# An order table of rounds for TensorE and VectorE in a fused attention and expert kernel

## The chip, the cores and the metric

The kernel runs on one core of one Trainium2 chip. The metric is the device time of one launch in microseconds, median of several runs. A profiled execution of the same program, in which the trace is recorded, stands beside it.

## What is computed

A batch of eight sequences of 1024 rows by 256 columns goes through a layer norm without weights, then through attention (16 heads of 16, rotary position) and through a layer of 8 experts in which each expert picks its own rows.

```python
def reference(x, ...):
    xn = _layernorm(x)
    return x + attention(xn, ...) + experts(xn, ...)

def attention(x, ...):
    z = layernorm(x) * ln_w + ln_b
    q, k, v = z @ Wq.T + bq, z @ Wk.T + bk, z @ Wv.T + bv      # heads of 16
    q, k = rope(q), rope(k)
    attn = softmax(q @ k.T / sqrt(16))
    return x + (attn @ v) @ Wo.T + bo

def experts(x, ...):
    affinity = softmax(x @ gate_w)                # 8 experts
    gating, index = top_k(affinity.T, 256)        # per sequence and expert
    h = silu(x[index] @ Wg) * (x[index] @ Wu)
    return zeros.at[index].add((h @ Wd) * gating)
```

## The kernel before

The program is written engine by engine, without a scheduler: each engine has its own list, and semaphores hold them together. A prologue prepares batch 0 (q, k, v and the routing for sequence 0). Then `attend` runs once for each of the eight sequences (batches here), and the experts follow in 32 units of 512 rows.

Within batch b, attention is 64 **steps** of two **pairs**. Step s has head group s // 16 (four heads), query half (s // 8) % 2 and key tile s % 8. A score pair is two matmuls, for two heads in two row lanes of the array (L985); it fills one of three `score` banks (RING), so pair p may be written only when the exponential of pair p - 3 is done. ScalarE takes one exponential per pair (L777, 1024 in all). The value product of a step (`weigh`, L999) multiplies all four heads' exponentials by the values and a column of ones; it is four matmuls, eight records in the trace. Eight steps accumulate in the only `o_ps` bank. After the eighth, VectorE copies it to `o_sb` (`copy_o`, L1475), and step 8k waits for that copy.

The order is counted in **cycles** of two steps. Cycle c issues scores of step 2c, product 2c - 2, scores of step 2c + 1, product 2c - 1; with a long job (q/k, v, output projection) in the cycle the two products go together between the scores. The products run two steps behind, so the last two of a batch are issued in cycle 0 of the next.

Between them TensorE prepares the next batch and finishes the previous one through **jobs**, each into the one `side` bank, from which VectorE takes it before the next job may start (`pe.wait_ge(side_free, jobs.before(job))`):

- ("z", half, c): four transposes of the normed rows (L852), ready when VectorE's norm3 is;
- ("logits", half) the router's logits (L859); ("square", half) head norms (L890) of squares that GpSimd makes (L667); ("peak",) a turn of the peaks (L899);
- ("qk", half, k) q and k projections (L868, six matmuls); ("v", pair) (L878); ("wo", quarter) the output projection of the previous batch (L909).

`NEXT_JOBS` and `PREV_JOBS` are dictionaries from a cycle to its job, 25 jobs a batch; batch 0 has no "wo" jobs, and `LAST_JOBS` has few, since no batch follows.

VectorE walks the same cycles (L1531). For the next batch it does, for each half, norm1 (first statistics, L1128, L1132), norm2 (`xn`, L1157 to L1137), stats2, norm3 (moments and `z`, L1173 to L1137); between them GpSimd raises the variance to the power -1/2 (L645). Later it does rotary products (L1261), rotary (L1277), split (high and low part of q and k, L1323, L1325). For the previous batch it does invert and the quarter splits (L1352 to L1495). All of it stands in one list with `copy_o` and the drains of the jobs. In the last batch VectorE runs 96 operations of top-k instead (`take_top`), four or five a cycle.

If a sequence's scores could overflow, a branch (`wide`) computes maxima first. It is not taken in this run.

Of the kernel before, what the change touches and what calls it, by code (L numbers as in the profile page):

```python
# [15 lines left out]
P = 128  # L16
# [100 lines left out]
def program(nc, ctx, g):  # L117
# [118 lines left out]
    def rows_ps(t):  # L236
# [65 lines left out]
    NEXT_JOBS = {4: ("z", 0, 0), 5: ("z", 0, 1), 6: ("logits", 0),  # L302
# [3 lines left out]
    SECOND_JOBS = {c + (c < 9): job for c, job in NEXT_JOBS.items()}  # L306
    PREV_JOBS = {9: ("wo", 0), 15: ("wo", 1), 23: ("wo", 2), 30: ("wo", 3)}
    LAST_JOBS = {0: ("top",), 9: ("wo", 0), 15: ("wo", 1), 23: ("wo", 2), 28: ("lists",), 30: ("wo", 3)}
    LONG_JOBS = ("qk", "v", "wo")
    END_JOBS = (("wo", 0), ("wo", 1), ("wo", 2), ("wo", 3))  # L310
    NFIRST, NNEXT = len(FIRST_JOBS), len(NEXT_JOBS) + len(PREV_JOBS)


    class Jobs:


        def __init__(self, base, by_cycle, order=None):
            self.base, self.by_cycle = base, by_cycle
            order = order or [by_cycle[c] for c in sorted(by_cycle)]
            self.offset = {job: i for i, job in enumerate(order)}  # L320
# [10 lines left out]
    def jobs_of(b):  # L331
# [3 lines left out]
        base = b * NNEXT + (NFIRST + len(NEXT_JOBS) - NNEXT)  # L335
        if isinstance(b, int) and b == NB - 1:
            return Jobs(base, LAST_JOBS)
        return Jobs(base, {**NEXT_JOBS, **PREV_JOBS})
# [12 lines left out]
    first_jobs = FirstJobs(0, None, FIRST_JOBS)  # L351
    NACT = sum(by_act(job) for job in FIRST_JOBS)
    last_jobs = jobs_of(NB - 1)
    end_jobs = Jobs(last_jobs.base + len(LAST_JOBS), None, END_JOBS)
# [490 lines left out]
    def _(pe):  # L845
# [48 lines left out]
        def turn_peaks(bank, n):  # L894
            pe.wait_ge(v_peaked, n + 1)
# [77 lines left out]
        def scores(b, s):  # L973
            hg, qh, kt = s // (2 * KT), (s // KT) % 2, s % KT
            par = hg % 2
            if b == 0 and s == KT // 2:
                pe.wait_ge(late_in[1], STACK_DMA // 2)
            elif b == 0 and s == KT:
                pe.wait_ge(late_in[0], STACK_DMA // 2)
            for i in range(NPAIR):  # L980
                p = NPAIR * s + i
                need(pe, exp_done, b * PAIRS + (p - RING + 1))
                for w in range(LANES):
                    rows = slice(w * LANE, w * LANE + FULL)
# [730 lines left out]
```

## Time and profile before

| | us |
|---|---|
| median of 3 runs | 1713.04 |
| lowest, highest | 1712.26, 1714.15 |
| span of the profiled execution | 1713.7 |
| busy in it: TensorE | 1667.3 (97%) |
| ScalarE | 1190.4 (69%) |
| VectorE | 1075.3 (63%) |
| GpSimd | 508.9 (30%) |
| first to last attention exponential | 59.5 to 1130.0 |

The profiled execution is 0.7 us above the median. Busy time of TensorE counts overlapping records, so that a share of 97% does not mean that it works at its peak; the chain of waits says what it waits for. In rows of the timeline and of groups, "x8" is the number of instructions, the figure before it the time that they cover.

### The profile page before, as it was taken

What the parts mean: (1) busy time and instruction counts of PE and PEld (TensorE: products, weight loads), DVE (VectorE), ACT (ScalarE), POOL (GpSimd) and SP (SyncE); (2) the same over time, 40 slices, a digit from 0 to 9 for tenths busy, and PEclk for the clock granted to TensorE, in tenths of its full rate; (3) what the DMA queues carried; (4) which work ended last, traced back from release to release, by engine and by line L of the source; (5) the groups of instructions that cost most, each with busy time, mean ns of one, the idle gap of its engine ahead of it and who ended that gap; (6) DMA issues with size and microseconds to landing.
All of it is one profiled execution on the core that took longest, in us unless ns stands there. A gap on an engine that the chain in (4) does not pass through costs nothing.

```text
span 1713.7 us, 29029 instructions
## 1 busy us (share of the span) xinstructions
PE 1667.3 (97%) x11128; PEld 947.8 (55%) x11128; DVE 1075.3 (63%) x2351; ACT 1190.4 (69%) x1416; POOL 508.9 (30%) x479
## 2 busy tenths in 40 slices
PE   5799999999999999999999999999999999999997
PEld 4234334333434433434434433368888888888886
DVE  7875487577477567558558658866555555454543
ACT  4698998998899899899898899953333333343322
POOL 3112101201111111112112100036566565656553
PEclk9799999999999999999999999999999999999999
DMA  5634754674574475465474566345444443534332
GB/s 168 173 60 122 162 116 106 174 145 106 134 169 122 115 156 143 116 142 138 118 161 104 118 134 140 59 152 117 86 93 66 92 92 66 99 62 96 65 56 31
DMA packets 113987, 196.08 MB, mean 114 GB/s; under 512 B 20896, under 2 KB 59680, under 8 KB 113696
## 3 DMA queue, kind: packets, MB, share of 16 engines
q1 hardware_dynamic: 83696, 143.01, 36.5%
q0 software_dynamic: 29040, 49.83, 15.0%
q8 instruction: 105, 1.72, 0.4%
q10 hardware_dynamic: 1088, 1.05, 0.2%
q14 instruction: 58, 0.48, 0.1%
HBM read 117.27 MB, written 76.55 MB: 113 GB/s over the span
## 4 chain that ended last, share of the span: by engine, by line
PE 93%; DVE 4%; DMA 1%; POOL 1%; issue 1%; ACT 0%; POOLq 0%; ACTq 0%; DVEq 0%
PE o_ps L999 28%; PE score L1079 20%; PE score L985 20%; PE side L868 5%; PE score L1091 5%; PE o_ps L1091 3%; PE side L878 3%; PE side L909 3%; PE side L1091 2%; PE score L1066 2%; PE side L852 1%; DMA probs<-in_wo_t 1%; PE side L859 0%; PE side L890 0%; POOL out L689 0%
## 5 line engine op out<-in xcount | busy, mean ns | idle before, releaser
L777 ACT ACTIVATE probs<-score 128x1024 f32<-128x1024 f32 x1024 | 967.8, 1063 | 105.5 <-PE score L985 103.3
L999 PE MATMUL o_ps<-probs,v_ones 128*32 128x512 f32 x4096 | 524.9, 605 | 1.8 <-DVE o_sb L1475 1.5
L985 PE MATMUL score<-q_stack,k_stack 50*128 50x512 f32 x2048 | 395.8, 458 | 4.0 <-issue 3.4
L985 PEld LDWEIGHTS score<-q_stack,k_stack 50*128 50x128 f32 x2048 | 164.0, 185 | 352.2 <-ACT probs L777 310.7
L761 ACT ACTIVATE probs<-score 128x512 f32<-128x512 f32 x128 | 76.6, 598 | 328.9 <-PE score L1079 328.9
L689 POOL DMA_INDIRECT out<-probs,rot x128 | 203.4, 1589 | 207.6 <-DVE probs L1440 178.3
L1425 DVE TENSOR_TENSOR probs<-score,probs 128x512 f32<-128x512 f32 x128 | 88.5, 691 | 205.3 <-PE score L1079 179.3
L999 PEld LDWEIGHTS o_ps<-probs,v_ones 128*32 128x32 f32 x4096 | 92.3, 108 | 201.1 <-issue 140.1
L667 POOL TENSOR_TENSOR square<-qk 128x512 bf16<-128x512 f32 x56 | 77.3, 1409 | 387.5 <-DVE qk L1278 387.5
L1079 PE MATMUL score<-k_stack,q_stack 128*128 128x512 f32 x640 | 158.6, 390 | 0.0
L678 POOL DMA_INDIRECT qk<-xn_rows,rot x128 | 132.0, 1031 | 38.3 <-issue 29.3
L1079 PE MATMUL score<-k_stack,zn_hi 128*128 128x512 f32 x512 | 139.9, 390 | 0.0
L1079 PEld LDWEIGHTS score<-k_stack,q_stack 128*128 128x128 f32 x640 | 119.1, 188 | 24.1
L1475 DVE COPY o_sb<-o_ps 128x512 f32<-128x512 f32 x64 | 44.3, 692 | 125.3 <-PE o_ps L999 125.3
L643 POOL TENSOR_SCALAR ve<-mv 128x4 f32<-128x4 f32 x32 | 8.3, 261 | 352.6 <-DVE mv L1132 352.6
L1079 PEld LDWEIGHTS score<-k_stack,zn_hi 128*128 128x128 f32 x512 | 95.0, 188 | 19.8 <-issue 0.8
L755 ACT CAST parts<-probs 128x512 fp32r<-128x512 f32 x128 | 78.6, 614 | 33.3 <-DVE probs L1425 33.3
L659 POOL COPY v_ones<-v_sb 128x512 f32<-128x512 f32 x32 | 19.7, 616 | 162.9 <-DVE v_sb L1347 85.9
L1417 DVE TENSOR_TENSOR w_hi<-probs,parts 128x512 fp32r<-128x512 f32 x96 | 65.4, 681 | 0.0
L1347 DVE TENSOR_TENSOR v_sb<-side,bv_sb 128x256 f32<-128x256 f32 x56 | 21.0, 416 | 68.9 <-PE side L878 68.9
L1440 DVE TENSOR_SCALAR probs<-score,rot 128x256 f32<-128x256 f32 x64 | 30.7, 483 | 52.1 <-PE score L1091 52.1
L1179 DVE COPY moments_of<-stats 32x2 f32<-32x2 f32 x224 | 46.2, 206 | 3.4
(282 smaller groups left out, 2546.9 us busy)
## 6 DMA issues: line engine op xcount, KB each, us to landing
q_parts<-parts SPq DMA_DIRECT2D x16, 1024.0 KB, 4.3
k_parts<-parts SPq DMA_DIRECT2D x16, 1024.0 KB, 7.4
q_stack<-q_parts SPq DMA_DIRECT2D x62, 256.0 KB, 7.2
k_stack<-k_parts SPq DMA_DIRECT2D x62, 256.0 KB, 8.7
q_stack<-q_parts SPq DMA_DIRECT2D x66, 128.0 KB, 7.6
k_stack<-k_parts SPq DMA_DIRECT2D x66, 128.0 KB, 8.3
o_sums<-o_sb SPq DMA_DIRECT2D x256, 32.0 KB
num<-o_sums SPq DMA_DIRECT2D x32, 256.0 KB
```

Source lines behind the costliest of these rows:

```text
L667: last = pool.tensor_tensor(square[i][:, :], qk[:, i, :], qk[:, i, :], ALU.mult)
L678: pool.indirect_dma_start(xs[par][:, t, :], None, xn_dram[:, :], bass.IndirectOffsetOnAxis(ap=rows_now[bp][:, t:t + 1], axis=0))\
L689: pool.indirect_dma_start(out[:, :], bass.IndirectOffsetOnAxis(ap=rows_now[bp][:, t:t + 1], axis=0), y[par][t], None, compute_op=ALU.add)\
L755: act.copy(h_hi[:, f, :], h[f % 2]).then_inc(h_high, 1)
L761: act.activation(silu[f % 2], g_ps[f % 2], ACT.Silu).then_inc(silu_done, 1)
L777: act.activation(probs[probs_of(b, s)][:, 2 * i:2 * i + 2, :], score[ring_of(b, p)][:, :, :], ACT.Exp, scale=SCALE).then_inc(exp_done, 1)
L868: last = pe.matmul(bank[:, :], wt[:, c, a * P:(a + 1) * P], zt[:, c, th * HALF:(th + 1) * HALF], start=i == 0 and c == 0, stop=i == 2 and ...
L985: last = pe.matmul(score[ring_of(b, p)][:, w, :], k_stack[par][rows, i, kt * P:(kt + 1) * P], q_stack[par][rows, i, qh * HALF:(qh + 1) * H ...
L999: last = pe.matmul(o_ps[j * KEYS_W:(j + 1) * KEYS_W, :], v_ones[par][:, kt, j, :], probs[probs_of(b, s)][:, j, :], start=kt == 0, stop=kt ...
L1079: last = pe.matmul(bank[f % 2], wt[k][w][:, c, f * P:(f + 1) * P], xt[:, c, :], start=i == 0 and c == 0, stop=i == 2 and c == DC - 1)
L1091: last = pe.matmul(rows_ps(t), ht, wt[k][DOWN][:, f, :], start=i == 0 and f == 0, stop=i == 2 and f == FC - 1)
L1425: dve.tensor_tensor(h[f % 2], u_ps[f % 2], silu[f % 2], ALU.mult).then_inc(h_done, 1)
```

## The change

One table replaces the cycles on both engines. An entry is a **round**: so many score pairs, so many products, and at most one job, issued in this order. Products still run two steps behind at a batch's start (LAG = 2), and 54 rounds make a batch.

```diff
-    NEXT_JOBS = {4: ("z", 0, 0), 5: ("z", 0, 1), 6: ("logits", 0),
-                 7: ("qk", 0, 0), 8: ("qk", 0, 1), 10: ("qk", 0, 2), 12: ("qk", 0, 3), 14: ("z", 1, 0), 16: ("z", 1, 1), 17: ("logits", 1), 18: ("square", 0),
...
+    NEXT_ROUNDS = ((3, 2), (2, 1), (3, 1), (1, 1), (3, 2), (3, 1, ("z", 0, 0)), (2, 1), (2, 1, ("z", 0, 1)), (3, 2),
+                   (2, 0, ("logits", 0)), (2, 2), (3, 0, ("qk", 0, 0)), (2, 2), (3, 2), (2, 0, ("qk", 0, 1)),
+                   (3, 2, ("wo", 0)), (3, 2), (3, 0, ("qk", 0, 2)), (2, 2), (3, 0, ("qk", 0, 3)), (0, 1), (3, 2),
...
+    FIRST_LATER = {("z", 0, 0): 7, ("z", 0, 1): 9, ("logits", 0): 10}
...
+            LAST_ROUNDS.append((NPAIR, 1, *{1: (("top",),), 57: (("lists",),)}.get(s, ())))
...
-    LOW_CYCLE = (28, 29, 30)
+    LOW_CYCLE = (29, 30, 31)
...
-    ROUTER_CYCLE = (9, 19)
+    ROUTER_CYCLE = (9, 20)
```

The rest of the table goes on in the same way: rounds of two or three pairs with two products, and rounds of two or three pairs with a job and no product. In all there are 38 groups of products (14 of one, 22 of two, 2 of three) where there were 48, and 51 groups of pairs (29 of three, 19 of two, 3 of one). Batch 0 takes the table without "wo" and with its first three jobs later; the last batch has rounds of two pairs and one product. TensorE:

```diff
-                scores(b, 2 * c)
-                grouped = c in jobs.by_cycle and jobs.by_cycle[c][0] in LONG_JOBS
-                weigh_past(b, 2 * c - 2, prev)
...
+            p, s = 0, -LAG
+            for entry in rounds_of(b):
+                for p in range(p, p + entry[0]):
+                    if p % GROUP_PAIRS == 0:
+                        open_group(b, p // GROUP_PAIRS, wide)
+                    score_pair(b, p)
+                p += entry[0] > 0
+                for s in range(s, s + entry[1]):
+                    weigh_past(b, s, prev)
+                s += entry[1] > 0
+                job = job_in(entry)
+                if job is not None:
                     pe.wait_ge(side_free, jobs.before(job))
                     run_job(jobs, job, nxt, prev, side[:, :])
```

VectorE walks the same rounds: in each, the copies of the output halves that end in it, then what belongs to the cycles whose first pair is in it, then the job's drain. Its work for the second half moves a cycle later (products 21 to 22, rotary 22 to 23, split 22 and 24 to 23 and 25), the peak of the values is taken in two halves, one scaling replaces two in `limits`, and the copy of the previous batch's last output half goes ahead of norm1.

```diff
+                for done in steps:
+                    if done >= 0 and done % KT == KT - 1:
+                        copy_o(b, done // KT)
+                    elif done == -1 and prev is not None:
                         copy_o(prev, 2 * NG - 1)
-                    stats2(nxt, 0)
...
+                for c in (at // (2 * NPAIR) for at in pairs if at % (2 * NPAIR) == 0):
+                    if nxt is None:
+                        alongside_last(b, prev, c)
+                    else:
+                        alongside(b, nxt, prev, jobs, c)
```

**VectorE at the start of a middle batch.** `xin` to `z` is the norm chain of the next batch, `o_sb<-o_ps` the copy of an output half. Before:

```order
L1128 BN_STATS stats<-xin 128x6 x4
L1132 BN_AGGR mv<-stats 128x2 x4
L1157 TENSOR_SCALAR grown<-rstd 128x4
L1158 SCALAR_TENSOR_TENSOR offset<-mv,rstd 128x4
L1137 TENSOR_SCALAR xn<-xin,mv,rstd 128x256 x4
L1475 COPY o_sb<-o_ps 128x512
L1128 BN_STATS stats<-xn 128x6 x4
```

Now:

```order
L1517 COPY o_sb<-o_ps 128x512
L1170 BN_STATS stats<-xin 128x6 x4
L1174 BN_AGGR mv<-stats 128x2 x4
L1199 TENSOR_SCALAR grown<-rstd 128x4
L1200 SCALAR_TENSOR_TENSOR offset<-mv,rstd 128x4
L1179 TENSOR_SCALAR xn<-xin,mv,rstd 128x256 x4
L1170 BN_STATS stats<-xn 128x6 x4
```

The copy has moved from behind norm2 to the head of the list.

**TensorE where step 47 ends an output half and step 48 begins the next,** in a middle batch, with buffer numbers (v_ones0 serves steps 32 to 47, v_ones1 steps 48 to 63). Before:

```order
L999 MATMUL o_ps<-probs1,v_ones0 32x512 x4
L999 MATMUL o_ps<-probs2,v_ones0 32x512 x4
L985 MATMUL score0<-q_stack1,k_stack1 128x512 x2
L985 MATMUL score1<-q_stack1,k_stack1 128x512 x2
L878 MATMUL side<-w_hi2,zn_hi 128x256 x2
L878 MATMUL side<-w_lo2,zn_hi 128x256 x2
L878 MATMUL side<-w_hi2,zn_lo 128x256 x2
```

Now:

```order
L1026 MATMUL score0<-q_stack1,k_stack1 128x512 x2
L1026 MATMUL score1<-q_stack1,k_stack1 128x512 x2
L1040 MATMUL o_ps<-probs2,v_ones0 32x512 x4
L1040 MATMUL o_ps<-probs0,v_ones1 32x512 x4
L1026 MATMUL score2<-q_stack1,k_stack1 128x512 x2
```

The two products on either side of the border, which had scores and a v job between them, now follow each other. The same holds for steps 23 and 24 and for 39 and 40.

**VectorE around the job ("z", 1, 1)** of a middle batch. Before:

```order
L1475 COPY o_sb<-o_ps 128x512
L1200 COPY xnT<-side 128x512
L1201 TENSOR_SCALAR znT<-side,lnw_sb,lnb_sb 128x512
L1207 CAST zn_hi<-znT 128x2x512
L1213 TENSOR_TENSOR zn_lo<-znT,zn_hi 128x2x512
```

Now:

```order
L1242 COPY xnT<-side 128x512
L1243 TENSOR_SCALAR znT<-side,lnw_sb,lnb_sb 128x512
L1249 CAST zn_hi<-znT 128x2x512
L1255 TENSOR_TENSOR zn_lo<-znT,zn_hi 128x2x512
L1517 COPY o_sb<-o_ps 128x512
```

The copy after step 31 has moved from ahead of the drain of the z job, with its two casts, to behind it.

## Rows read from the trace of the kernel before

**Rows 1.** Busy time by stretch: batch 0, a middle batch (3), the last; columns in the first line

```profile
core 0: us, PE busy (x) PEld busy (x) DVE busy (x) ACT busy (x) POOL busy (x), PEclk, DMA share, GB/s
59.48:194.86 135.38, 133.31 (x914) 49.64 (x915) 86.81 (x210) 121.03 (x130) 22.70 (x26) 0.96 0.52 119
466.39:602.17 135.78, 135.78 (x976) 55.17 (x972) 89.77 (x219) 121.68 (x132) 22.34 (x25) 1.00 0.57 134
1009.46:1129.96 120.50, 119.22 (x820) 39.19 (x812) 99.40 (x219) 118.37 (x129) 10.00 (x11) 1.00 0.48 103
```

**Rows 2.** The chain of waits, cycles 4 to 9 of batch 3: start us, length us, what

```profile
487.57 0.59 PE side L852 x4
...
490.48 1.00 PE o_ps L999 x8
...
491.91 0.66 PE score L985 x4
492.57 1.85 PE o_ps L999 x16
...
495.09 1.59 PE side L868 x6
...
504.63 1.57 PE side L909 x12
```

**Rows 3.** The chain of waits, cycle 2 of batch 3

```profile
476.33 0.84 PE score L985 x4
```

**Rows 4.** VectorE's timeline, start of batch 3: start, length, work, [idle before <-releaser]

```profile
464.18 1.41 DVE L1128 BATCH_NORM_STATS2 stats<-xin 128x6 f32<-128x256 f32 x4 [0.29 <-issue]
...
467.49 0.17 DVE L1157 TENSOR_SCALAR grown<-rstd 128x4 f32<-128x4 f32 x1 [1.49 <-POOL rstd L645]
...
476.89 1.38 DVE L1137 TENSOR_SCALAR z<-xn,mv,rstd 128x256 f32<-128x256 f32 x4
```

**Rows 5.** Timelines of TensorE and VectorE where batch 5's first output half is copied

```profile
739.47 1.06 PE L999 MATMUL o_ps<-probs,v_ones 128*32 128x512 f32 x8
...
741.34 1.06 PE L999 MATMUL o_ps<-probs,v_ones 128*32 128x512 f32 x8
...
740.60 0.69 DVE L1475 COPY o_sb<-o_ps 128x512 f32<-128x512 f32 x1 [0.70 <-PE o_ps L999]
```

**Rows 6.** VectorE's timeline, the drain of a second z job

```profile
488.19 0.69 DVE L1200 COPY xnT<-side 128x512 f32<-128x512 f32 x1 [2.46 <-PE side L852]
...
490.36 1.23 DVE L1213 TENSOR_TENSOR zn_lo<-znT,zn_hi 128x1024 fp32r<-128x1024 f32 x1
```

**Rows 7.** VectorE's timeline from a quarter split to norm3 and the rotary products

```profile
499.87 0.88 DVE L1352 SCALAR_TENSOR_TENSOR base<-base,grown,bo_sb 128x256 f32<-128x256 f32 x2
...
502.45 0.74 DVE L1252 TENSOR_SCALAR qk<-side,bq_sb 128x512 f32<-128x512 f32 x1
...
515.42 0.68 DVE L1261 TENSOR_TENSOR rot<-qk,cos_sb 128x512 f32<-128x512 f32 x1
```

**Rows 8.** Start of batch 0: TensorE and VectorE timelines, and busy time with PEclk

```profile
80.80 1.28 PE L999 MATMUL o_ps<-probs,v_ones 128*32 128x512 f32 x8 [1.49 <-DVE o_sb L1475]
...
78.77 1.38 DVE L1137 TENSOR_SCALAR z<-xn,mv,rstd 128x256 f32<-128x256 f32 x4
...
80.66 3.90 DVE L1194 TENSOR_REDUCE gate_sum<-base 128x8 f32<-128x2048 f32 x1
...
81.00:85.00 4.00, 4.00 (x20) 0.70 (x12) 3.56 (x1) 2.44 (x3) 0.00 (x0) 0.57 1.00 242
```

**Rows 9.** SyncE's timeline (last load of batch 4's first stack), and the page's DMA issues

```profile
585.51 0.42 SPq L461 DMA_DIRECT2D k_stack<-k_parts  x1
...
k_stack<-k_parts SPq DMA_DIRECT2D x62, 256.0 KB, 8.7
```

**Rows 10.** VectorE's timeline, the last batch: two top-k steps of eight

```profile
1013.45 0.69 DVE L1525 MAX8 top_gate<-znT 128x8 f32<-128x512 f32 x1
...
1015.77 0.69 DVE L1525 MAX8 top_gate<-znT 128x8 f32<-128x512 f32 x1
```

More of the change, by code:

```diff
@@ new lines, in first_rounds @@
+    def first_rounds():
+        moved = []
+        for r, entry in enumerate(NEXT_ROUNDS):
+            job = job_in(entry)
+            later = [j for j, at in FIRST_LATER.items() if at == r]
+            job = later[0] if later else None if job in FIRST_LATER or job is not None and job[0] == "wo" else job
+            moved.append(entry[:2] if job is None else (*entry[:2], job))
+        return moved
+    FIRST_ROUNDS = first_rounds()
+    NEXT_JOBS, SECOND_JOBS, LAST_JOBS = ([job_in(entry) for entry in rounds if len(entry) == 3]
+                                         for rounds in (NEXT_ROUNDS, FIRST_ROUNDS, LAST_ROUNDS))
@@ L1529, in take_top, with alongside, alongside_last @@
                 dve_t.mark(dve.match_replace(top_scores, top_gate[:, eight], top_scores, -1.0))
+        def alongside(b, nxt, prev, jobs, c):
+            if prev is not None:
+                splits = LAST_SPLIT_CYCLE if nxt is None else SPLIT_CYCLE
+                if c == 7:
+                    invert(prev, 1)
+                if c in splits:
+                    quarter_split(prev, splits.index(c))
+            elif c == 4:
+                sum_gate()
+            if c == 0:
+                norm1(nxt, 0)
+                norm2(nxt, 0)
+                stats2(nxt, 0)
+            elif c in (1, 10):
+                norm3(nxt, c // 10)
+            elif c == 6:
+                norm1(nxt, 1)
+            elif c == 9:
+                norm2(nxt, 1)
+                stats2(nxt, 1)
+            elif c in (11, 22):
+                products(jobs, c // 22, 0)
+            elif c in (12, 23):
+                rotary(0)
+            elif c in (14, 24):
+                products(jobs, c // 24, 1)
+            elif c in (15, 25):
+                rotary(1)
+            elif c in (28, 30):
+                value_peak(jobs, c // 30)
+            elif c == 31:
+                invert(b, 0)
+            if c in (13, 22):
+                affinities(nxt, c // 22)
+            if c in (13, 23):
+                split(nxt, c // 23, 0)
+            elif c in (15, 25):
+                split(nxt, c // 25, 1)
+        def alongside_last(b, prev, c):
+            if c == 7:
+                invert(prev, 1)
+            if c in LAST_SPLIT_CYCLE:
+                quarter_split(prev, LAST_SPLIT_CYCLE.index(c))
+            for op in range(TOPS_DONE[c], TOPS_DONE[c + 1]):
+                take_top(op)
+            if c == LISTS_CYCLE:
+                order_lists()
+            if c == 30:
+                invert(b, 0)
+            if c in LOW_CYCLE:
+                if c == LOW_CYCLE[0]:
+                    dve.wait_ge(parts_out, NB * 2 * PARTS_DMA)
+                first_cast(LOW_CYCLE.index(c))
+                low_weights(0, LOW_CYCLE.index(c))
         def attend(b, nxt, prev):
@@ L1597, in _ @@
+                job = job_in(entry)
+                if job is not None:
+                    take(jobs, job, nxt, prev, side[:, :])
         dve.memset(peaks[:, :], 0.0).then_inc(zeros_set, 1)
@@ L1649, in _ @@
         first("v", 3)
-        value_peak(first_jobs)
+        value_peak(first_jobs, 0)
+        value_peak(first_jobs, 1)
         first_low(1, 1)
```

177 lines of the change are left out of this document (69 added, 108 removed), and 3 rows, old and new, of tables (NEXT_JOBS, NEXT_ROUNDS).

## The prediction

> **What bounds the kernel now.** I read the stretches of the batches first. A middle batch takes 135.8 us, the first 135.4, the last 120.5 [rows 1]. In a middle batch TensorE is marked busy all the time, ScalarE for 121.7 us. Matmul records overlap, so that mark proves nothing by itself; the chain of waits does. In cycles 4 to 9 of batch 3 it runs through TensorE alone: two score pairs 0.66 us, one value product 1.00, two in one go 1.85, a projection job 1.59, and no exponential between them [rows 2]. TensorE's own order is the bound there. In the first cycles of a batch, which have no job, two pairs hold the chain for 0.84 us instead of 0.66 [rows 3]: ScalarE sets the pace there. That happens in eight or nine half cycles, 1.6 us a batch.
>
> Check by addition for a middle batch: 128 pairs by 0.33, 42.4; 32 single products by 1.00 and 16 double ones by 1.85, 61.6; eight q/k jobs by 1.59, four output jobs by 1.57, four v jobs of as many matmuls of the same size, and nine short jobs of at most 0.59, about 30; waits 1.6. Together 135.6, measured 135.8. So there is little to win: all that TensorE loses to others today is 1.6 us.
>
> **The parts, for a middle batch (1 to 6).**
>
> Fewer groups of products. A product that follows another costs 1.85 - 1.00 = 0.85 us instead of 1.00 [rows 2]. 48 groups become 38: 10 x 0.14 = **-1.4 us**. Score pairs cost 0.33 each in a group of two, and no row shows a third; bounds 0.33 (the pairs before it) and 0.13 (half the 0.26 us a matmul of the q/k job, since the two lanes run side by side). I take 0.33, the same operation, so groups of three give nothing. The Trainium skill (TensorE: Matmul & The Clock Gate, section Back-to-back issue gap) puts the gap of matmuls in a stream at N/2.4 + 2.5 ns, 216 ns for 512 columns; by it the third pair would save 0.12 us, 29 times, and the sum would be 3.4 us a batch lower. No pair in the trace is that cheap.
>
> The first z job. The copy of the last output half (step -1) now stands ahead of norm1 in VectorE's list. Today norm1 starts at 464.18, 2.2 us before the batch's first exponential [rows 1, 4], and z is done at 476.89 + 1.38 = 478.27: 14.1 us, of which 0.6 are the copy in between; one of two waits for GpSimd's powers is the 1.49. After the change the copy waits for step -1: three pairs (1.0), a first product (0.86), the second's 1.06 to its end, a semaphore (0.07), the copy (0.6). So norm1 starts 3.6 us after the batch's first score and z is ready at 3.6 + 13.5 = 17.1. TensorE comes to ("z", 0, 0) after 15 pairs (5.0), eight products in six groups (two of 1.85, four of 1.00: 7.7) and about 0.6 of exponential waits, at 13.3. Wait **+3.8** (3 to 4.3). Today the job stands in cycle 4, behind 20 pairs, and z is ready before it. Behind the waiting job stand only scores, so ScalarE runs dry too, but it has 14 us a batch to spare.
>
> Output halves that end inside a group. There is one o_ps, so step 8k starts only when VectorE has copied it after step 8k - 1. Today at least two pairs lie between. Where just these do, the rows show the shortest way: product at 739.47, copy 740.60 to 741.29, next product 741.34, 1.87 us from start to start [rows 5]. In the new order steps 23 and 24, 39 and 40, 47 and 48 stand in one group, where the second would start after 0.86. 1.87 - 0.86 = 1.0, three times: **+3.0**, and more where VectorE is busy at that moment. This is the surest term.
>
> Step 32. From the start of job ("z", 1, 1) TensorE has that job 0.59, a pair 0.33, steps 30 and 31 1.85, three pairs 1.0: 3.8 us to step 32. VectorE drains the job from 0.7 on, with both casts 3.4 [rows 6], and only then copies: 0.7 + 3.4 + 0.7 = 4.8. **+1.0** (0 to 1.2).
>
> ("qk", 0, 3) waits for the drain of ("qk", 0, 2). From the start of ("qk", 0, 1), TensorE needs 15.0 us to come to it: two q/k jobs (3.2), one output job (1.6), 14 pairs (4.6) and three double products (5.6). VectorE has just begun a quarter split then (499.87 to 502.45, 2.6), followed by a drain, norm2, stats2, wo's sum, norm3, another drain and the four rotary products (502.45 to 516.10, 13.6) [rows 7]; in the new order the products stand ahead of the second drain, so that this one ends last: 16.3. **+1.3** (0 to 2).
>
> The clock. In batch 0 TensorE stood idle for 1.49 us until 80.80, and over the next four microseconds (81 to 85) the granted clock was 0.57, most of it at 1.2 GHz instead of 2.4: 4 x 0.43 = 1.7 us lost [rows 8]. In a middle batch it is 1.00 throughout [rows 1]. The wait for z leaves TensorE idle for 3.5 us; I take the same drop behind it, **+1.7** (0 to 3.4).
>
> At nothing: the second half's products, rotary and split move one VectorE cycle later, so q and k of the next batch go out through SP's queue up to 4 us later. The last load of the next first stack is issued at 585.51 and takes 8.7 us [rows 9], the batch's first exponential is at 602.17: 8 us of cover. If it were gone the batch would start late. GpSimd's squares come later by as much, and so does their job. The peak of the values in halves, and one scaling instead of two, lie on an idle VectorE.
>
> Sum: -1.4 + 3.8 + 3.0 + 1.0 + 1.3 + 1.7 = **+9.4** a batch, +56 in six.
>
> Batch 0: no previous copy, so z is done at 80.15 as now. gate_sum (cycle 4, 3.90 us) now stands ahead of the copy after step 7, so that one ends at 84.7 and step 8 starts then instead of at 80.80 [rows 8], with one short job more behind it: +3.4. Then the borders 3.0, step 32 0.9, two drains 3, exponentials where no output job fills the time 2, groups -1.4: **+11**.
>
> Last batch: VectorE's copies now follow cycle 4k's five top-k operations, 2.32 us for three [rows 10], 3.9 us a cycle against 3.7 of TensorE's pace. Waits of 1 to 2 us at steps 8, 24 and 40, partly caught up: **+3** (0 to 5). The experts stay.
>
> 56 + 11 + 3 = +70 on the profiled 1713.7; the median is 0.7 lower than that span, so **1783 us**.
>
> **Rivals.**
> 1. Faster: VectorE's copy and z are not what comes last. TensorE keeps the -1.4, and spread jobs win back the 1.6 of exponential waits: -3.0 x 6, 1695 us. It decides whether step 24 starts 0.86 us after step 23 and z comes before 13.3 us. For it: VectorE is busy only 90 us of 136. Against: the copy needs step 8k - 1, and no free VectorE makes the 1.87 shorter.
> 2. The same waits, but the clock stays: 7.7 x 6 + 14 = +60, 1773.
> 3. Only what the order itself forces: z 3.0, borders 3.0, groups -1.4, so 4.6 x 6 + 5 = +33, 1746. VectorE's lateness elsewhere would have to vanish.
> 4. A third pair is cheap: if the array runs on once a group streams, at 0.21 instead of 0.33, 3.4 us a batch come back, 24 in all: 1759. Against it every pair of the trace. It is also what the skill's figure above would give.
> 5. VectorE falls behind in earnest, borders cost 1.5 each and stacks land late: over 1802.
>
> **Numbers.** Forecast 0.50, rival 2 0.22, rival 3 0.08, rival 4 0.04, rival 5 0.07, rival 1 0.06, and 0.03 that gains and waits cancel within 0.2%, about what a measurement can tell from no change. The range 1745 to 1802 holds the forecast, 2, 3, 4 and the bounds. Faster 0.06, same 0.03, slower 0.91.
>
> **What would show it.** A middle batch of 143 to 146 us, the surplus in four places: TensorE idle some 3.5 us about 13 us into each batch, ended by VectorE's z; three times 1.0 us of o_ps waiting for the copy; a clock under 1.0 just after the z wait; the q/k drain at about 52 us. The last batch 121 to 125. The prediction is wrong if z is ready at 13 us, if the copies end before TensorE asks, or if three pairs take under 0.9 us.

## The result

| | us | against the kernel before |
|---|---|---|
| before, median of 4 runs | 1713.51 (1712.26 to 1714.15) | |
| changed, median of 4 runs | 1781.43 (1776.49 to 1784.46) | ratio 1.0388, 95% interval 1.0375 to 1.0400 |
| changed, profiled execution | 1782.51, span 1780.4 | |

The change makes the kernel 68 us slower. Busy time by stretch of the changed kernel, cut where each batch issues its first exponential, as in [rows 1]: batch 0, batch 3, the last batch, the experts behind it.

```profile
core 0: us, PE busy (x) PEld busy (x) DVE busy (x) ACT busy (x) POOL busy (x), PEclk, DMA share, GB/s
56.67:206.85 150.18, 134.73 (x910) 53.30 (x907) 85.32 (x202) 121.26 (x130) 22.49 (x24) 0.92 0.47 107
495.71:638.95 143.24, 134.21 (x976) 56.35 (x972) 90.55 (x220) 121.38 (x131) 22.62 (x24) 0.99 0.56 127
1068.94:1194.08 125.14, 121.31 (x822) 39.53 (x820) 98.57 (x219) 119.07 (x128) 9.56 (x11) 0.97 0.46 99
1194.08:1780.36 586.28, 570.88 (x3392) 504.19 (x3392) 303.74 (x501) 198.15 (x342) 334.08 (x281) 0.99 0.43 84
```

Batch 0 is 14.8 us longer, batch 3 7.5, the last 4.6. Batches 1 to 6 together are 47.5 us longer (8.9, 8.4, then 7.5 to 7.6 four times). ScalarE has the same work, 121.4 us in batch 3; TensorE has the same instructions, but its busy time fell from all of the batch to 134.2 of 143.2. For the rest it now stands still. The page of the profile says for whom: the lines of its costliest groups over the whole run, with the idle time before them at the end of a line.

```profile
L819 ACT ACTIVATE probs<-score 128x1024 f32<-128x1024 f32 x1024 | 968.5, 1040 | 173.2 <-PE score L1026 169.0
L1040 PE MATMUL o_ps<-probs,v_ones 128*32 128x512 f32 x4096 | 521.6, 611 | 28.7 <-DVE o_sb L1517 28.7
```

Before, ScalarE's exponentials stood idle for 105.5 us in all and the products for 1.8. TensorE in batch 3, by groups with idle time; then its timeline at the places of [rows 5] and of the sum:

```profile
L1040 PE MATMUL o_ps<-probs,v_ones 128*32 128x512 f32 x512 | 64.3, 607 | 3.4 <-DVE o_sb L1517 3.4
L1026 PE MATMUL score<-q_stack,k_stack 50*128 50x512 f32 x260 | 46.3, 444 | 0.4 <-ACT probs L819 0.2
L910 PE MATMUL side<-zn_hi,w_hi 128*128 128x512 f32 x16 | 5.8, 446 | 1.4 <-DVE qk L1294 1.4
```

```profile
495.11 0.97 PE L1026 MATMUL score<-q_stack,k_stack 50*128 50x512 f32 x6
...
507.30 1.07 PE L1040 MATMUL o_ps<-probs,v_ones 128*32 128x512 f32 x8
512.23 0.63 PE L894 MATMUL side<-ident_sb,z 128*128 128x128 f32 x4 [3.86 <-DVE z L1179]
...
549.73 0.73 PE L910 MATMUL side<-zn_hi,w_hi 128*128 128x512 f32 x2 [1.38 <-DVE qk L1294]
...
553.21 1.07 PE L1040 MATMUL o_ps<-probs,v_ones 128*32 128x512 f32 x8
555.09 1.07 PE L1040 MATMUL o_ps<-probs,v_ones 128*32 128x512 f32 x8 [0.81 <-DVE o_sb L1517]
```

The first z job waits 3.86 us for VectorE, from 13.3 to 17.1 us after the batch's first score at 495.11. ("qk", 0, 3) waits 1.38 for the drain of ("qk", 0, 2). Steps 23 and 24 start 1.88 us apart instead of 0.86, with the copy between them; steps 39/40 and 47/48 do the same, and step 32 comes 0.84 us late. VectorE at the start of the batch, which answers to [rows 4]:

```profile
498.00 0.69 DVE L1517 COPY o_sb<-o_ps 128x512 f32<-128x512 f32 x1 [1.91 <-PE o_ps L1040]
498.61 1.39 DVE L1170 BATCH_NORM_STATS2 stats<-xin 128x6 f32<-128x256 f32 x4
...
510.70 1.38 DVE L1179 TENSOR_SCALAR z<-xn,mv,rstd 128x256 f32<-128x256 f32 x4
```

Norm1 follows the copy, and z is done 13.5 us after norm1 began, as the prediction had it. The clock behind that wait, by stretch: in the 4 us of waiting TensorE was busy for 0.77 us at full clock, then it worked at half of it.

```profile
509.00:513.00 4.00, 0.77 (x6) 0.63 (x8) 3.03 (x15) 0.86 (x1) 0.00 (x0) 1.00 1.00 154
513.20:516.40 3.20, 3.20 (x16) 0.70 (x12) 1.10 (x2) 1.94 (x2) 0.00 (x0) 0.50 1.08 233
```

One thing in the chain of waits is cheaper than the prediction took it. Start, length, work, around 560 and 611 us:

```profile
558.40 0.90 PE score L1026 x6
...
563.90 0.66 PE score L1026 x4
...
611.80 2.71 PE o_ps L1040 x24
```

Three pairs hold TensorE for 0.90 us, two for 0.66: the third costs 0.24, not 0.33. Three products take 2.71, each further one 0.86.

### The profile page after: what moved, and what is told of

Same layout as the page of the kernel before. It is cut to its first block, busy times and chain, and to the rows that moved or that the text cites. A ratio compares the mean times of both kernels' runs of the same rounds, so it can differ in the third digit from the quotient of the medians.

```text
span 1780.4 us, 29029 instructions
## 1 busy us (share of the span) xinstructions
PE 1664.7 (94%) x11128; PEld 960.4 (54%) x11128; DVE 1079.8 (61%) x2351; ACT 1190.0 (67%) x1416; POOL 515.4 (29%) x479
## 4 chain that ended last, share of the span: by engine, by line
PE 74%; DVE 18%; ACT 3%; issue 2%; POOL 2%; DMA 1%; another core or an unknown queue 0%; ACTq 0%; POOLq 0%; DVEq 0%
PE o_ps L1040 20%; PE score L1121 19%; PE score L1026 13%; PE score L1133 5%; PE side L910 4%; PE o_ps L1133 3%; DVE moments_of L1221 3%; PE side L920 3%; PE side L1133 2%; ACT probs L819 2%; DVE o_sb L1517 2%; DVE stats L1170 2%; PE side L951 2%; PE score L1108 1%; POOL rstd L687 1%
## 5 line engine op out<-in xcount | busy, mean ns | idle before, releaser
L1026 PE MATMUL score<-q_stack,k_stack 50*128 50x512 f32 x2048 | 377.9, 453 | 9.8 <-ACT probs L819 4.2
L1026 PEld LDWEIGHTS score<-q_stack,k_stack 50*128 50x128 f32 x2048 | 170.5, 189 | 316.7 <-ACT probs L819 249.1
L1040 PEld LDWEIGHTS o_ps<-probs,v_ones 128*32 128x32 f32 x4096 | 97.9, 109 | 253.5 <-issue 140.3
L1121 PE MATMUL score<-k_stack,zn_hi 128*128 128x512 f32 x512 | 140.2, 390 | 1.2 <-DVE probs L1467 1.2
L1517 DVE COPY o_sb<-o_ps 128x512 f32<-128x512 f32 x64 | 44.2, 690 | 134.7 <-PE o_ps L1040 131.7
L701 POOL COPY v_ones<-v_sb 128x512 f32<-128x512 f32 x32 | 25.2, 787 | 194.9 <-DVE v_sb L1389 111.9
L1294 DVE TENSOR_SCALAR qk<-side,bq_sb 128x512 f32<-128x512 f32 x28 | 21.0, 748 | 61.8 <-PE side L910 61.8
```

The lines of the kernel that those rows point to most:

```text
L1026: last = pe.matmul(score[ring_of(b, p)][:, w, :], k_stack[par][rows, i, kt * P:(kt + 1) * P], q_stack[par][rows, i, qh * HALF:(qh + 1) * H ...
L1040: last = pe.matmul(o_ps[j * KEYS_W:(j + 1) * KEYS_W, :], v_ones[par][:, kt, j, :], probs[probs_of(b, s)][:, j, :], start=kt == 0, stop=kt ...
L1121: last = pe.matmul(bank[f % 2], wt[k][w][:, c, f * P:(f + 1) * P], xt[:, c, :], start=i == 0 and c == 0, stop=i == 2 and c == DC - 1)
L1517: dve.tensor_copy(o_sb[il % 2][:, :], o_ps[:, :]).then_inc(o_copied, 1)
```

## The experiments

The theory: four kinds of waits that the new order puts on TensorE, and the clock behind one of them, make the 68 us. Rivals: the walk of a table costs by itself; the waits are VectorE's lateness and would stand elsewhere; filled time comes back as waits for exponentials. Each kernel ran beside the kernel before on its chip (medians there 1712.7 to 1715.4); batch lengths come from its one profiled execution.

**e1, the old order in the new code.** The table of the middle batches spells out the old cycles, and a helper fills the tables of batch 0 and of the last batch in the same way. VectorE's work goes back to its old cycles too, but for a few operations: the copy ahead of norm1, the value peak in two halves and the one scaling stay as changed. The 11128 matmuls of TensorE come in the order of the kernel before.

```diff
+    def by_cycles(at):
+        rounds = []
+        for c in range(STEPS // 2):
+            job = at.get(c)
+            both = job is not None and job[0] in ("qk", "v", "wo")
+            rounds += [(2, 2 if both else 1), (2, 0 if both else 1) + (() if job is None else (job,))]
+        return rounds
```

> The changed kernel with its table filled so that TensorE issues exactly the order of the kernel before (every matmul in the same place); the walk through a table, the value peak in two halves and VectorE's copy of the last product group ahead of the norm stay as the change has them. Theory (the order of the rounds costs the 68 us): 1713 us within 4, middle batches at 135.7 us as before, against 143.3 with the new table; the copy ahead of norm1 may hold z back by about 1 us, but the z job stands behind cycle 4 there and has that time. Rival (the table's code, or VectorE's new order, costs by itself): 1745 us or more, middle batches at 140 or more.

Measured: 1717.69 us (10 runs), ratio 1.0015 (1.0006 to 1.0025). Busy time of batch 3:

```profile
464.28:600.04 135.76, 135.76 (x976) 55.20 (x972) 90.05 (x219) 121.67 (x132) 21.58 (x24) 1.00 0.59 134
```

Batches take 135.3, 135.8 six times and 120.5, the old lengths to 0.1 us, though VectorE's copy stands ahead of norm1 here too and norm1 starts at 467.56, 3.3 us into the batch:

```profile
467.56 1.39 DVE L1179 BATCH_NORM_STATS2 stats<-xin 128x6 f32<-128x256 f32 x4
```

The table, its code and the early copy cost the batches nothing: where the job stands in cycle 4, z has the time. The loss lies in the two orders that e1 puts back, that of the rounds and that of VectorE's other work along them. e1 does not tell these two apart; e4, and batch 0 of e7, do. The median is 2.5 us above the kernel beside it, clear of the noise. In the profile that time stands outside the batches, which together are 0.2 us shorter than before.

**e2, the z jobs later.** In rounds 7, 9 and 10 in place of 5, 7 and 9 (only the entries that change, out of their lines):

```diff
-                   (3, 1, ("z", 0, 0)), (2, 1), (2, 1, ("z", 0, 1)), (3, 2), (2, 0, ("logits", 0)), (2, 2),
+                   (3, 1), (2, 1), (2, 1, ("z", 0, 0)), (3, 2), (2, 0, ("z", 0, 1)), (2, 2, ("logits", 0)),
```

> In the table of the middle batches the jobs z(0,0), z(0,1) and the first logits move from rounds 5, 7 and 9 to rounds 7, 9 and 10, where batch 0 has them already; all else stays. Theory (TensorE comes to z 3.9 us too early, 12.2 us into a batch where z is there at 17.1, and its clock then falls to 0.5 for 3.4 us, worth 1.6 us): the wait of 4.9 us falls to 1.6 or less, the stretch at clock 0.5 goes, and a drain wait of up to 1.5 us in front of qk(0,0) may come: 2.5 to 5.5 us less for each of the six middle batches, 15 to 33 in all, 1757 us (1748 to 1766). Rival (the time before z is filled with work that is missing later, so exponentials or the copy end the next wait): the same 1781 within 4. Rival (the clock falls without the wait as well): z's part alone, 10 to 15 us, 1769.

Measured: 1758.46 us, 1.0250 (1.0233 to 1.0267). TensorE's groups in batch 3 that wait for VectorE, then the z jobs:

```profile
L910 PE MATMUL side<-zn_hi,w_hi 128*128 128x512 f32 x16 | 5.8, 446 | 2.7 <-DVE znT L1262 1.4 <-DVE qk L1294 1.4
L894 PE MATMUL side<-ident_sb,z 128*128 128x128 f32 x16 | 2.6, 287 | 0.0
```

The wait for z is gone, the clock stays at 1.00, and 1.4 us came back in front of ("qk", 0, 0), which now stands right behind the logits: middle batches 140.1, 3.2 less (3.9 and 1.5 come back and 1.4 goes; of the 0.8 left the trace marks 0.2 as a wait for an exponential, the rest is open). Batch 0 and the last batch have the same instructions as in the changed kernel and took 151.0 and 122.7 us against 150.2 and 125.1; so the lengths of those two differ by 1 to 2 us from one execution to the next.

**e3, the borders.** At steps 23/24, 39/40 and 47/48 the last product of an output half and the first of the next go to different rounds, in batch 0 too (only the entries that change):

```diff
-(0, 1), (3, 2)
+(0, 2), (3, 1)
-(3, 3), (3, 0, ("qk", 1, 1)), (2, 2)
+(3, 2), (3, 0, ("qk", 1, 1)), (2, 3)
-(2, 2), (2, 0, ("v", 0))
+(2, 1), (2, 0, ("v", 0)), (0, 1)
```

> Three entries of the table are cut so that no two products of one round lie on both sides of a product group's end (steps 23 and 24, 39 and 40, 47 and 48): the first product of the new group goes to the next round, with a round of score pairs between. Theory (TensorE waits 1.0 us at each of the three for VectorE's copy of the finished group): three waits of 1.0 us go in each of the seven batches with this table, less up to 1 us of waits for exponentials that come in their place: 2 to 3 us per batch, 14 to 21 in all, 1765 us (1760 to 1769). Rival (the copy is late because VectorE is busy, wherever the product stands): no more than 5 us, 1776 to 1781.

Measured: 1768.87 us, 1.0307 (1.0289 to 1.0324), 12.6 less than the changed kernel. Batches 3 and 4 and the waits of batch 4:

```profile
487.49:630.14 142.65, 135.85 (x976) 57.22 (x972) 90.63 (x220) 120.86 (x131) 22.60 (x24) 0.98 0.57 129
630.14:771.24 141.10, 134.30 (x976) 56.73 (x972) 90.51 (x220) 120.87 (x131) 22.59 (x24) 0.99 0.55 127
```

```profile
L1040 PE MATMUL o_ps<-probs,v_ones 128*32 128x512 f32 x512 | 64.0, 608 | 0.9 <-DVE o_sb L1517 0.9
```

The wait for the copy falls from 3.4 to 0.9 us (step 32's is left), 2.2 us a batch where the clock was low for 3.4 us as before. In four of the six the low stretch behind z lasted 6.8 us and took 1.5 of it back. The time is in the expected range, the gain of 12.6 us just under its 14 to 21, the mechanism the expected one.

**e4, VectorE's order alone.**

```diff
+                late = NPAIR if nxt is None else 0
-                for c in (at // (2 * NPAIR) for at in pairs if at % (2 * NPAIR) == 0):
+                for c in (at // (2 * NPAIR) for at in pairs if at % (2 * NPAIR) == late):
...
-            elif c == 4:
+            elif c == 5:
                 sum_gate()
```

> Two orders on VectorE alone, TensorE's table untouched: in the last batch the top-k, the splits and the low weights of a cycle come one round later, so behind the copy of a product group that ends there and not ahead of it; in batch 0 the sum of the gate (3.9 us) moves from cycle 4 to cycle 5, behind the first copy. Theory (the walk of the table puts these ahead of the copies: waits of 1.3, 1.6 and 1.2 us before steps 8, 24 and 40 of the last batch, 1.9 us before step 8 of batch 0): the last batch falls from 125.1 to 121.5, batch 0 from 150.2 to 148.3, total 1776 us. Rival (the last batch is longer since its wo jobs come one cycle later): last batch stays at 125, total 1779 to 1781.

Measured: 1776.18 us, 1.0353 (1.0335 to 1.0370). Batch 0 and the last batch:

```profile
56.42:204.55 148.13, 135.50 (x910) 53.32 (x907) 85.52 (x202) 121.33 (x130) 22.47 (x24) 0.93 0.48 109
1065.12:1185.33 120.21, 119.97 (x822) 39.44 (x820) 98.79 (x219) 118.42 (x128) 9.54 (x11) 1.00 0.48 103
```

2.1 and 4.9 us less: the last batch is back at its old length, with its output jobs where the change put them. Its loss was the top-k ahead of the copies. The products of the last batch, in the changed kernel and in e4, and the clock behind the second of its three waits (1.09, 1.46 and 1.07 us):

```profile
L1040 PE MATMUL o_ps<-probs,v_ones 128*32 128x512 f32 x512 | 69.1, 618 | 3.6 <-DVE o_sb L1517 3.6
L1040 PE MATMUL o_ps<-probs,v_ones 128*32 128x512 f32 x512 | 67.4, 604 | 0.0
```

```profile
1120.50:1127.40 6.90, 6.90 (x32) 1.90 (x28) 6.66 (x16) 3.88 (x4) 0.00 (x0) 0.51 0.68 218
```

The same last batch, with the same three waits, took 122.7 us in e2, where the clock stayed, and 123.8 in e5, where it was low for 3.4 us; so by these some 2.5 us of the 4.9 are the waits and the rest is the clock. Of batch 0, the trace of e4 shows that the wait before step 8 is gone (1.6 us in the changed kernel, 2.1 in e2, 2.8 in e5). The 2.1 us of its length prove less, since e5, which leaves batch 0 alone, has 148.4 us too.

**e5, z one round later.** ("z", 0, 0) in round 6, nothing else.

> Only the job z(0,0) of the middle batches moves, by one round (5 to 6); z(0,1) and the logits stay in rounds 7 and 9. TensorE should come to it 1.7 us later than in the changed kernel (a single product and two pairs), about 14 us into the batch, so that a wait of 1.6 to 3.2 us stays before z, and qk(0,0) keeps its place behind the logits. Theory (a wait of 4.9 us on z takes the clock to 0.5; waits of about 1.8 us, as those before qk in the last study's runs, don't): the wait is 1.6 to 3.2 us, the clock stays at 1.0, the middle batches take 139.5 to 141 us and the whole about 1760 us (1755 to 1767). Rival (any wait on z takes the clock down): batches of 141.5 to 143, 1768 to 1778 us.

Measured: 1766.09 us, 1.0318 (1.0299 to 1.0337). Batches 2 and 3, and the wait for z, which is 1.7 us in both:

```profile
346.35:486.58 140.23, 133.15 (x976) 56.24 (x972) 90.70 (x220) 121.15 (x131) 22.39 (x24) 1.00 0.57 130
486.58:628.21 141.63, 134.55 (x976) 56.82 (x972) 90.62 (x220) 121.18 (x131) 22.61 (x24) 0.99 0.57 129
```

```profile
L894 PE MATMUL side<-ident_sb,z 128*128 128x128 f32 x8 | 1.3, 283 | 1.7 <-DVE z L1179 1.7
L894 PE MATMUL side<-ident_sb,z 128*128 128x128 f32 x6 | 1.3, 336 | 1.7 <-DVE z L1179 1.7
```

Neither theory is right alone. (The wait that the text above puts at 4.9 us measured 3.9, and what it says of waits of 1.8 us in another study stands in no run here.) Behind the same wait the clock fell in four of the six middle batches (141.6 to 142.0 us) and stayed in two (140.2 and 140.0). This prices the low stretch: 1.4 to 1.6 us for 3.4 us at half clock. The 3.9 us wait of the changed kernel brought it down in every middle batch, the 1.4 us in front of ("qk", 0, 0) in e2 in none of the six. The profiled execution is the fastest of e5's four; the slower ones have a lower mean clock (0.981 in the two slowest against 0.986), so that there the clock fell more often or for longer.

**e6, e2, e3 and e4 together.**

> The edits of e2, e3 and e4 in one kernel. Theory (they end separate waits, each of TensorE's own time): the gains add, 1781.4 less 23.0 (e2), 12.6 (e3) and 5.3 (e4) = 1740.5 us, within 5; middle batches at 137.9 us (143.3 less 3.2 and 2.2), the last batch at 120 to 121, batch 0 at 144 to 146. Rival (where one wait goes the next takes up the time, so that the gains overlap): 1750 us or more.

Measured: 1736.42 us, 1.0139 (1.0123 to 1.0154), five middle batches 137.9 to 138.0 and batch 1 139.9, last 120.2, batch 0 143.5. The gains add. By the text's sum 4.1 us more came back than expected, but that sum sets runs of different sessions against each other, and the kernel before was 1713.5 us beside the changed kernel, 1715.2 beside e2 to e4 and 1712.7 beside e6. Each against its own kernel before, the changed kernel is 67.9 us slower, and the gains are 24.7 (e2), 14.3 (e3) and 6.9 (e4), 45.9 together against 44.2 in e6. Of the middle batches' loss 2.1 us each is left: in batch 3 TensorE still waits 1.4 us before each of two q/k jobs and 0.8 before step 32.

**e7, a new table.** For the middle batches; batch 0 takes the old order, VectorE is as in e4. Its start:

```diff
+    NEXT_ROUNDS = ((3, 2), (3, 2), (3, 1), (2, 1), (2, 1), (2, 1), (1, 1), (3, 1, ("z", 0, 0)), (2, 1, ("z", 0, 1)),
+                   (3, 2, ("logits", 0)), (3, 0, ("qk", 0, 0)), (2, 2), (2, 0, ("qk", 0, 1)), (3, 1), (0, 2),
...
```

> A table written anew for the middle batches from the waits read so far: z(0,0) in round 7 and the logits two rounds later, every product group's first product (steps 8, 16, ... 56) in another round than the last of the group before with at least two score pairs between, and at least 1.5 us of other work (a product and pairs) between the last of one long job and the start of the next; batch 0 takes the order of the kernel before, with the peak one cycle later; the last batch as in e4. 37 or 38 groups of products against 48. Theory (the changed kernel's idea is worth its 10 groups at 0.14 us each once no wait is added, and the waits of the old order's job drains go as well): middle batches at 133 to 135 us against 135.8, batch 0 at 135.5, last 120.3: 1703 us (1696 to 1710), faster than both. Rival (three pairs in a row overrun ScalarE, whose exponentials then set the time): waits for exponentials of 0.3 us and more in each of the dozen rounds with three pairs, batches at 136 or more, 1713 to 1725 us.

Measured: 1722.26 us, 1.0049 (1.0035 to 1.0062), middle batches 136.0 to 138.5. The theory missed by 3 us a batch. The rival's numbers hold, but of its reason only half: ScalarE's exponentials in batch 3:

```profile
L816 ACT ACTIVATE probs<-score 128x1024 f32<-128x1024 f32 x128 | 121.7, 1033 | 15.5 <-PE o_ps L1037 7.5 <-PE score L1023 7.4
```

Half of ScalarE's idle time is now for products: probabilities have three buffers, so the first exponential of step s waits for product s - 3. ScalarE stands 0.6 to 0.7 us there, and TensorE then 0.4 to 0.5 for the exponential. There are four such places in a batch, not a dozen. The other waits of batch 3, 0.45 and 0.47 us, are for VectorE's drains before ("wo", 3) and a q/k job; peak itself, which the next text names, does not wait.

```profile
521.49 0.50 PE L1023 MATMUL score<-q_stack,k_stack 50*128 50x512 f32 x2 [0.42 <-ACT probs L816]
...
602.56 0.51 PE L948 MATMUL side<-w_hi,at_hi 128*128 128x256 f32 x2 [0.45 <-DVE terms L1340]
```

Batch 0 tells something more. In e7 it has TensorE's old order (with peak one cycle later) and VectorE's new one (with the gate's sum behind the copy), and it takes 135.2 us, the old length. There VectorE's new order costs nothing by itself. As far as batch 0 speaks for the middle ones, what they lose comes from the rounds.

**e8, e9, e10, three more tables.** Each puts right what the last one's trace showed (e10 differs from e9 by peak alone, one round ahead).

> The table of e7 written again with what its trace showed: in e7's middle batches (137.4 us) ScalarE stood 0.6 us before an exponential four times, each for a value product three steps back that had not yet read its probabilities, and the peak job came 0.5 to 0.9 us too early. Here no first pair of a step is issued before that product has had its time, and peak stands one round later; 40 groups of products against 36 in e7 and 48 in the kernel before. Batch 0 and the last batch as in e7. Theory (these five waits are all that e7 had over a batch without waits): middle batches at 134.0 to 134.6 us, 137.4 less 3.1; in all 1722.3 less 6 x 3.1 = 1703.7 us (1699 to 1709), faster than the kernel before. Rival (a batch cannot be shorter than the 135.8 of the old order, since its 48 groups already hid their price under ScalarE): middle batches at 135.5 or more, 1712 us or more.

Measured: 1730.11 us, 1.0092 (1.0076 to 1.0107). Middle batches of 136.6, but also 140.5 and 139.8: as slow as the rival had it, but not since the old order's groups were free. VectorE's groups over them:

```profile
L1391 DVE SCALAR_TENSOR_TENSOR base<-base,grown,bo_sb 128x256 f32<-128x256 f32 x48 | 20.9, 476 | 16.5 <-DMA base<-in_x 16.5
```

The quarter split waits for the next base from memory, and ("wo", 0) for the drain behind that: 0.95 us at 499.94, 3.09 at 225.29. The second squares wait 1.1 us more in every middle batch.

> Once more a new table for the middle batches, with what e8's trace showed: there wo(0) came 31.8 us into the batch, but the split of the quarter that it needs waits on VectorE for the rows of the next base, whose transfer lands 27 to 32 us into the batch and not at one time; so TensorE waited 1.0 to 3.2 us for VectorE, and once more 1.2 us for the second squares. Here wo(0) comes 36 us in or later and the squares two cycles after the rotary; 42 groups of products. Batch 0 and the last batch as in e7 and e8. Theory (a table can be had without these waits, but the room for them takes back most of what fewer groups give: 6 groups at 0.14 us are 0.8 us a batch): middle batches at 135.0 to 135.8 us, batch 1 within 2 us of them, in all 1708 to 1716 us, the same as the kernel before within 0.2 per cent. Rival (the new order of the walk on VectorE always leaves it late somewhere): middle batches above 136.5, 1719 us or more.

Measured: 1750.63 us, 1.0205 (1.0190 to 1.0219), batches of 139 to 142: the rival's numbers, which had a lower bound only. VectorE and TensorE at the end of batch 3:

```profile
612.33 0.55 DVE L1519 RECIPROCAL den_rec<-den 128x64 f32<-128x64 f32 x1 [9.76 <-DMA den<-o_sums]
...
613.52 0.80 PE L948 MATMUL side<-w_hi,at_hi 128*128 128x256 f32 x2 [4.49 <-DVE terms L1340]
```

VectorE is not full there: it stands 9.8 us at the reciprocal of cycle 31 for a transfer; the drain of peak is queued behind it, and ("wo", 3) behind the drain.

> The table of e9 with one job moved by one round: peak goes from the round behind the first pair of cycle 31 to the one ahead of it. In e9 VectorE came to the reciprocal of the denominators, which belongs to cycle 31, before the drain of the peak job, and stood 9.8 us there for the transfer of the denominators; TensorE waited 3.9 to 4.6 us before wo(3) for that drain, and its clock then fell for 3.4 to 6.8 us. Theory (that one place is all that made e9's batches 142 us long): the wait before wo(3) goes, the clock stays up, middle batches at 135.5 to 136.5 us, at most 0.5 us of it a new wait before peak, the whole 1711 to 1718 us, within 0.2 per cent of the kernel before. Rival (the drain is late because VectorE is full at the end of a batch, wherever the job stands): batches at 139 us or more, 1735 us or more.

Measured: 1718.46 us (11 runs), 1.0033 (1.0024 to 1.0042), batches 135.9 to 137.5. One job moved by one round gave 32 us between the medians, 30 when each is set against the kernel before on its own chip (1715.4 and 1713.1 us): the wait and the low clock are gone. It ends just above the expected range; z waits 0.4 us in batch 3 and 1.2 in batch 4, the second squares 0.5 to 0.6 in every middle batch.

**e11, e12, two last tables.**

> A last table for the middle batches, with all that the runs before showed kept apart: each place where VectorE's drain, z, the second squares, peak or the rows of the base ended TensorE's wait gets 0.3 to 1 us more room, and peak stands ahead of cycle 31's reciprocal. 44 groups of products and 53 of score pairs, against 48 and 64 in the kernel before and 38 and 51 in the changed one. What fewer groups give is read anew from the trace of the changed kernel: a score group costs 0.43 us with one pair, 0.66 with two and 0.90 with three, so each group saved gives 0.19 us, and each group of products saved 0.14: 11 x 0.19 + 4 x 0.14 = 2.6 us a batch, less waits for exponentials of 1.7 us that the kernel before has too and 1 us more. Theory: middle batches at 134.2 to 135.3 us, in all 1706 to 1713 us, the first version a little faster than the kernel before. Rival (the time of a transfer that VectorE waits for, the base or the denominators, moves by some us from batch to batch and ends in a wait of TensorE wherever the order is this tight): batches at 136 or more, 1716 us or more.

> The same aims as e11 with another order: 42 groups of products and 49 of score pairs, so 15 x 0.19 + 6 x 0.14 = 3.7 us a batch less for groups, but more waits for exponentials, some 3.5 us in nine places against 1.7 us in the kernel before. Theory: middle batches at 134.6 to 135.8 us, in all 1708 to 1716 us. Rival as for e11: batches at 136.5 or more, 1719 us or more.

Measured: e11 1708.82 us, 0.9971 (0.9960 to 0.9982); e12 1705.66 us, 0.9955 (0.9941 to 0.9968). Batches 3 and 4 of e12, then batch 4 of e11:

```profile
461.21:595.76 134.55, 132.72 (x976) 56.20 (x972) 89.87 (x221) 121.19 (x130) 21.62 (x24) 1.00 0.60 136
595.76:731.11 135.35, 132.82 (x976) 56.11 (x972) 89.83 (x220) 121.39 (x131) 21.62 (x24) 1.00 0.59 135
```

```profile
598.18:733.00 134.82, 133.58 (x976) 55.91 (x972) 90.66 (x219) 120.75 (x131) 22.98 (x24) 1.00 0.58 135
```

Both beat the kernel before, by 4.9 us (0.29%, as expected) and 8.0 us (0.45%, more than expected): little, but clear of the noise. e12 beats the changed kernel by 76 us. The code is the changed kernel's but for batch 0's table and the few lines of e4. Its middle rounds:

```python
    NEXT_ROUNDS = ((3, 2), (2, 2), (3, 1), (3, 1), (1, 1), (3, 0), (1, 2), (3, 1, ("z", 0, 0)), (3, 1, ("z", 0, 1)),
                   (3, 2, ("logits", 0)), (3, 2, ("qk", 0, 0)), (3, 1, ("qk", 0, 1)), (3, 2), (3, 0, ("wo", 0)),
                   (2, 1), (2, 2), (3, 2), (3, 0, ("qk", 0, 2)), (2, 2), (2, 1), (2, 0, ("qk", 0, 3)), (2, 2),
                   (3, 1, ("z", 1, 0)), (0, 1), (3, 1, ("wo", 1)), (3, 1, ("z", 1, 1)), (2, 1),
                   (2, 1, ("logits", 1)), (3, 2), (3, 1, ("square", 0)), (2, 2), (3, 0, ("qk", 1, 0)), (0, 1),
                   (3, 2), (2, 0, ("qk", 1, 1)), (3, 2, ("qk", 1, 2)), (3, 1, ("qk", 1, 3)), (3, 1, ("wo", 2)),
                   (3, 3), (3, 0, ("v", 0)), (2, 1, ("v", 1)), (3, 2), (2, 2), (3, 0, ("v", 2)), (2, 2), (3, 2),
                   (2, 0, ("v", 3)), (3, 2), (2, 1, ("square", 1)), (3, 1, ("peak",)), (2, 2), (2, 0, ("wo", 3)))
```

## Why the prediction was right, term by term

The forecast was 1783 us, slower; measured 1781.43. The terms of a middle batch, against batch 3 of the two traces (sums over TensorE's groups, from each group's start to the next one's):

| term | predicted | measured |
|---|---|---|
| product groups 48 to 38 | -1.4 | -1.2 |
| score pairs, 64 groups to 51 | 0 | -2.5 |
| wait for z | +3.8 | +3.9 |
| three borders | +3.0 | +3.1 |
| step 32 | +1.0 | +0.8 |
| ("qk", 0, 3) | +1.3 | +1.4 |
| clock | +1.7 | +1.5 |
| more waits for exponentials | 0 | +0.5 |
| sum | +9.4 | +7.5 |

The surplus of 7.5 us was right in its places, and the largest were moved by experiments: e2 took out the wait for z with the clock behind it, e5 told the clock apart from the wait, e3 took out the borders. One term was mis-sized: "I take 0.33, the same operation, so groups of three give nothing". Of its two ends, 0.33 and 0.13, the value was nearer the middle. A score group costs 0.43 us with one pair, 0.66 with two and 0.90 with three, thus 42.5 us before and 3 x 0.43 + 19 x 0.66 + 29 x 0.90 = 40.0 after. The mechanism of rival 4 was therefore real, at 2.5 us a batch and not 3.4, though its time of 1759 us did not come: no row gave its 0.21. The third pair of a group starts 0.234 us after the second. The second starts 0.337 after the first in both kernels, which is why the trace before could not show it. By the prediction's own sign (wrong if three pairs take under 0.9 us) this term stood right at the edge. The Trainium skill (TensorE: Matmul & The Clock Gate, section Back-to-back issue gap) gives 216 ns for 512 columns as the gap of an isolated matmul and 131 ns as the sustained one. The prediction took the first for that of a stream; the 0.234 us of a third pair, which is two matmuls in two row lanes, lie near it all the same.

The total came closer than its parts did, and that was luck: the six middle batches were 8.9 us less than their 56.4, the two outer ones 5.4 us more than their 14. The forecast's last step, from span to median, had an offset of its own: the changed kernel's profiled execution took 2.1 us more than its span, while the forecast set the median 0.7 us under the span. Span against span the change is +66.7 against the forecast's +70. **Batch 0** is +14.8 against +11. The line "z is done at 80.15 as now" was right for VectorE, 20.6 us into the batch, but TensorE now asks 3.3 us before that, which the sum left out, as it did the clock behind it (low for 23 us of the batch against 12 before). The timelines of TensorE and VectorE, and the clock behind, which answer to [rows 8]:

```profile
77.44 1.08 PE L894 MATMUL side<-ident_sb,z 128*128 128x128 f32 x4 [3.31 <-DVE z L1179]
81.74 3.64 PE L1040 MATMUL o_ps<-probs,v_ones 128*32 128x512 f32 x16 [1.64 <-DVE o_sb L1517]
...
77.21 3.88 DVE L1236 TENSOR_REDUCE gate_sum<-base 128x8 f32<-128x2048 f32 x1
```

```profile
82.00:86.00 4.00, 4.00 (x20) 0.89 (x12) 1.00 (x2) 0.15 (x1) 0.00 (x0) 0.50 0.25 70
```

The wait for the copy of step 7 is 1.64 us and not 3.4 longer than before, as the z wait had already given VectorE that time. The mean clock of the batch is 0.92 instead of 0.96. **The last batch** is +4.6 against +3, in the range given. e4 shows the cause, the three waits of 3.6 us in sum, and that about 2 us of the loss are the clock, which the sum had left out here too. **Batches 1 and 2** have 1.4 and 0.9 us more than the rest, with 6.8 us of low clock. Beside the terms stand the experts, +2.5 us, and the time to the first exponential, -2.8. Neither belongs to the table: the experts' stretch was 583.8 to 591.1 us long over the fourteen profiles, with the same instructions in all, and e1, in the old order, started its first exponential at 57.4 us. The three longest of them (589.3 to 591.1) also have the most time at low clock, 12.0 to 14.6 us against 7.9 to 10.9 in the others, which at half clock can explain some 2 of the 5 us between them and the rest. What else moves these two is open.

Rival 1 (VectorE's copy and z are not last) falls by e2 and e3, rival 2 by the clock of 0.50, rival 3 since step 32, the drain and the clock are there, rival 5 since the borders cost 1.0 and no stack came late. Not tried: step 32 and ("qk", 0, 3) alone. They are read from the trace only.

## What to carry to other kernels

An order written as a table is as good as its entries: nearly the same code ran 1705.7 and 1781.4 us. Price a switch between two kinds of matmul on both sides (here 0.19 us a score group and 0.14 a product group), but pay for it with slack at every place where another engine hands something over: the last product of an accumulator and the next first one want other work between them, a job wants the time of the drain before it, and buffers three deep tie the first engine to the second. On the draining engine, what waits for a transfer must not stand ahead of what another engine waits for; one such place, moved by one round, was worth 30 us. Change the order, read which wait ends last, and put right that one: the tables went 1781, 1722, 1730, 1751, 1718, 1709, 1706.

## What was not expected of the hardware

The third score pair of a group starts 0.234 us after the second (median of 173 groups in the six middle batches, never under 0.226), the second 0.337 after the first (never under 0.334). A wait of 3.9 us on TensorE always brought the clock to half here, for 3.4 or 6.8 us. Shorter ones sometimes do and sometimes do not, in the same code: 1.7 us did in four of six batches of e5; 1.46 us did in the last batch of the changed kernel and 1.45 in the same place of e2 did not; 1.38 us did in batch 0 of e1, and 1.4 us before ("qk", 0, 0) in none of the six middle batches of e2. And a transfer that VectorE needs (the rows of the base) let it go on at 29.0 to 31.6 us into the batch in one execution of e8, which a tight table turns into waits of 0.9 to 3.1 us on TensorE; in the kernel before it had cost VectorE 0.2 us in all those batches and TensorE nothing.
